# A perceiver layer on one core: the drain of the token loop without its 56 filler products

## The reference

```python
x = x + xattn(layernorm(x), ctx, ctx)   # 16 heads of 16, softmax(q k^T) v, output projection
x = x + attn(layernorm(x))              # rms norm, rotary q and k, sigmoid weights / their sum, v, projection
x = x + ffn(layernorm(x))               # one expert of 8 for each token, capacity 160 an expert, gelu, gate weight
```

## Time and profile before

| | us |
|---|---|
| median of 3 executions | 1117.71 |
| lowest, highest | 1116.65, 1118.75 |
| the profiled execution, its own time | 1113.46 |
| its span, first to last instruction | 1111.5 |
| its mean granted TensorE clock | 0.991 of full |
| PE, DVE, ACT, POOL busy in the span | 1073.4, 880.0, 798.7, 245.1 |
| the drain on PE, from the first hold to the first transposed row | 988.5 to 1020.3 |
| the experts, from there to the last product | 1020.3 to 1102.9 |

### The profile page before, as it was taken

The page is one execution under the profiler, slowest core; times in us unless marked ns, Lnnn a source line. Parts: engine busy times, 40 slices in busy tenths (PEclk is TensorE's granted clock), DMA queues, the critical chain, the costliest instruction groups (busy, mean ns, idle before and its releaser), DMA issues.

```text
span 1111.5 us, 40833 instructions
## 1 busy us (share of the span) xinstructions
PE 1073.4 (97%) x16195; PEld 875.3 (79%) x16195; DVE 880.0 (79%) x2650; ACT 798.7 (72%) x2319; POOL 245.1 (22%) x521
## 2 busy tenths in 40 slices
PE   6899999999999999999999999999999999988996
PEld 4678777878888888887887888888887788766996
DVE  6678888888888888888888888888888888774211
ACT  5677777887877877877888787787787787742221
POOL 1011122222222222222222222222222222221111
PEclk9899999999999999999999999999999999999998
DMA  4452522222212221122222211122112221001673
GB/s 137 115 149 55 200 67 69 69 65 62 62 46 58 59 63 54 45 59 60 62 61 60 61 58 43 55 59 57 44 52 58 58 60 36 17 12 44 211 244 109
DMA packets 71100, 82.04 MB, mean 74 GB/s; under 512 B 16427, under 2 KB 49916, under 8 KB 70912
## 3 DMA queue, kind: packets, MB, share of 16 engines
q1 hardware_dynamic: 64896, 75.06, 23.2%
q0 software_dynamic: 3360, 3.72, 1.0%
q10 hardware_dynamic: 2656, 0.66, 0.3%
HBM read 64.79 MB, written 16.56 MB: 73 GB/s over the span
## 4 chain that ended last, share of the span: by engine, by line
PE 85%; issue 4%; DVE 3%; DMA 3%; SPq 2%; ACT 1%; POOL 1%; POOLq 0%; DVEq 0%; ACTq 0%
PE vps L423 16%; PE kps L411 14%; PE score L457 9%; PE score L443 7%; PE gather L470 6%; PE shared L479 5%; PE shared L494 4%; PE shared L533 4%; PE score L766 3%; PE score L752 3%; PE shared L518 3%; PE shared L400 2%; PE score L485 2%; PE score L502 2%; SPq L266 1%
## 5 line engine op out<-in xcount | busy, mean ns | idle before, releaser
L818 ACT ACTIVATE prob<-score,nmx 128x257 f32<-128x257 f32 x512 | 236.2, 477 | 92.0 <-DVE nmx L1070 91.9
L411 PE MATMUL kps<-ctx_p,wk_p 128*128 128x512 f32 x768 | 217.3, 412 | 0.5 <-DVE wk_p L1056 0.4
L423 PE MATMUL vps<-wv_p,ctx_p 128*128 128x256 f32 x1536 | 215.7, 290 | 0.8 <-issue 0.8
L1070 DVE TENSOR_REDUCE nmx<-score 128x2 f32<-128x514 f32 x256 | 165.3, 688 | 54.6 <-PE score L443 54.6
L423 PEld LDWEIGHTS vps<-wv_p,ctx_p 128*128 128x128 f32 x1536 | 191.9, 190 | 15.2 <-issue 13.8
L411 PEld LDWEIGHTS kps<-ctx_p,wk_p 128*128 128x128 f32 x768 | 138.2, 190 | 38.7 <-issue 13.7
L1081 DVE TENSOR_SCALAR prob<-prob,rsum 128x256 f32<-128x256 f32 x512 | 159.4, 354 | 9.1
L1537 POOL TENSOR_TENSOR rstd<-ve,const 128x1 f32<-128x1 f32 x64 | 52.9, 826 | 464.4 <-DVE ve L1199 234.9
L457 PE MATMUL score<-const,prob 128*128 128x128 f32 x1024 | 147.1, 276 | 5.3 <-DVE prob L1081 5.0
L457 PEld LDWEIGHTS score<-const,prob 128*128 128x128 f32 x1024 | 115.6, 142 | 9.0 <-DVE prob L1081 7.6
L1062 DVE SCALAR_TENSOR_TENSOR ctx_p<-ctxT,nlast,ctx_p 128x256 fp32r<-128x256 f32 x256 | 111.8, 478 | 8.2 <-ACT ctx_p L835 8.2
(11 more groups left out here) (226 smaller groups left out, 1757.7 us busy)
## 6 DMA issues: line engine op xcount, KB each, us to landing
ctxT<-in_ctxT SPq DMA_DIRECT2D x128, 257.0 KB, 3.2
w<-in_w SPq DMA_DIRECT2D x16, 1024.0 KB, 8.8
xq<-in_x SPq DMA_DIRECT2D x32, 128.0 KB, 2.1
xr<-in_x SPq DMA_DIRECT2D x32, 128.0 KB
qbd<-qkT SPq DMA_DIRECT2D x248, 16.0 KB, 1.8
out<-row SPq DMA_DIRECT2D x31, 128.0 KB, 3.1
slots<-row SPq DMA_DIRECT2D x10, 257.0 KB, 5.7
x_a<-slots SPq DMA_DIRECT2D x8, 129.0 KB, 2.1
```

Of the source, the lines that this page charges most:

```text
L411: last = mm(kps[:, :], wk_p[:, x, n, c * P:(c + 1) * P], ctx_p[:, y, n, 2 * r:2 * r + 2, :].rearrange("p j s -> p (j s)"), start=(n, x) == ...
L423: last = mm(vps[:, c, :], ctx_p[:, x, n, j, c * P:(c + 1) * P], wv_p[:, y, n, :], start=(n, x) == (0, LO), stop=(n, y) == (C - 1, LO))
L818: last = af(prob[:, m, :], score[:, m, 0:S], ACT.Exp, bias=nmx[:, m:m + 1], scale=1.0, accum_out=esum[:, m:m + 1])
L1070: v.tensor_reduce(nmx[:, 2 * c:2 * c + 2], score[:, 2 * c:2 * c + 2, 0:S], AX.X, ALU.max, negate=True).then_inc(s["max_done"], 1)
```

## The change

The eight counts are set to zero, so that `hold` issues nothing. No wait, semaphore, buffer or other instruction changes.

```diff
-HOLDS = (12, 5, 2, 4, 5, 1, 3, 24)
+HOLDS = (0, 0, 0, 0, 0, 0, 0, 0)
```

## The result

| | before | after |
|---|---|---|
| median (lowest to highest), 6 executions each | 1117.08 (1113.02 to 1118.75) | 1125.97 (1123.54 to 1127.69) |
| ratio, 95% interval | | 1.0068 (1.0048 to 1.0087) |
| the profiled execution, its span | 1113.46, 1111.5 | 1127.69, 1125.6 |
| mean granted clock | 0.991 | 0.970 |

The kernel without the 56 products is slower, by 7.6 us by the ratio (5.4 to 9.7). The median lies 0.3 us above the top of the range that I gave (1125.7); the ratio, applied to the 1117.71 us that the range was built on, gives 1125.3, inside it. In the last series of experiments the changed kernel was timed again beside the other, six executions: 1.0060 (1.0038 to 1.0083), which is 6.7 us. Four executions in the experiments took 5% longer or more (1177.62, 1185.93, 1192.03 and 2948.37 us), and the ratios leave them out.

What follows compares the result with a forecast made beforehand. PE was taken to bound the token loop and, without cover, the experts; the drain alternates between engines. Terms -0.7 + 1.3 + 1.6 + 2.3 = +4.5 us, carried to the median, gave 1122.2 us; 8-in-10 range 1118.7 to 1125.7.

Steps and rivals of the forecast that it cites:

- Time given back by the holds: Drain and wait before the experts: removing the 56 unread products returns their time, -0.7 us (-0.2 small places, -0.5 last 24).
- 0.5 us comes back: Last 24 products, before expert 0's transposes: rows land by 1019.7, plus 0.1 us signal, so PE could start 0.5 us earlier.
- The projection at the lower level: Query and key projection behind y1 in the drain: clock falls to 1.2 GHz, 2.93 us instead of 1.64, +1.3 us.
- The rest of the drain: Values, self scores, outputs and gates behind the projection: +3.2 us if the clock stays low throughout, half taken, +1.6.
- low from y1 to the end: Rival: rest of drain too thin to lift the clock, which rises late in the experts too; +6.8 us, 1124.5 us, chance 0.14.
- The projection and the values are dense enough to lift it again: Step for the drain behind y1: clock returns there, then thin pieces lower it, so half of 3.2 us was taken.
- The first expert: Expert 0 begins at 1.2 GHz after over 6 us of idle PE: transposes +0.5, products +1.8 over 4 us, together +2.3.
- the main case: Clock low in a part of the drain and at expert 0's start: 1122.2 us, own range 1119.8 to 1124.3, chance 0.60.
- SP's load: Sign: the load of the 32 rows (line 348), before the experts, comes 2 to 4 us later.
- Only the last pause counts: Rival: clock stays up in the drain and falls only ahead of the experts; +1.6 us, 1119.3 us, chance 0.17.
- The holds don't keep the clock: Rival: clock behaves alike in either kernel, drain and experts only get time back; -0.7 us, 1117.0 us, chance 0.06.
- Faster: Rival: holds delay the chain before the experts; at most -8.3 us, 1109.4 us; chance 0.03 for over 0.2% faster.

## Why the prediction was right or wrong

**Direction and order of size: right.** Slower with a chance of 0.77, by clock and not by work; it forecast +4.5, the ratio says +7.6 (5.4 to 9.7), the second one +6.7. Three terms were wrong, all of them the same way, too low, so nothing cancelled. The range held because its upper end took in the price of the low clock throughout, though I had given that case 0.14. By terms, against the two traces of the changed kernel:

- *Time given back by the holds, -0.7.* Wrong, it is 0 where a run can tell. The step that failed is "0.5 us comes back" from the last 24. I took the DMA's 164 KB by 1019.7 for the landing, and 0.1 us for the signal, which no run shows. The signal comes later: with nothing in PE's way it is 1.97 us from the issue of the load to the first transpose, with the 24 in the way 2.02. The Trainium skill (DMA: Bandwidth & Descriptors, on the anatomy of one DMA) says of the other path of issue, GpSimd's, that most of a fixed 2.0 us is the confirmation behind the last byte; on SP's path the sum is like it here, 1.97 us, but less than half of it lies behind the traffic: 0.6 us from the 164 KB to the transpose in the kernel before, some 0.5 in the changed one. Of the three places flush with their successors the first gave nothing either: y1 is transposed 3.2 us after the positions in both. The other two can't be read, since the clock is low there.
- *The projection at the lower level, +1.3.* Right: 2.90 us against 1.64.
- *The rest of the drain, +1.6 as half of 3.2.* The price was near, the half was the error. The clock was low through all of it, as in the rival "low from y1 to the end", to which I gave 0.14. In the first trace the self scores start 2.05 us later than before, of which the projection is 1.3 and the rest 0.8, as worked out. The two together cost 0.9 more (I had 0.7), output A until the start of output Z 1.0 more, with DVE now waiting 0.77 us for PE (I had 0.5, with idle time behind it as cover), from there to gate Z 0.9, and 0.4 to the last positions. That is 3.9 for my 3.2. The sentence that failed is "The projection and the values are dense enough to lift it again". They didn't in either trace of the changed kernel, nor with only the last 24, where the clock came back 24.2 us into the drain and for 3.4 us only. With the five products of place 1 right behind the projection it came back 10.8 us into the drain (all but the first 12).
- *The first expert, +2.3.* Too small, it is +3.6 and +3.1. The transposes cost 0.45 as worked out, the products 2.6 instead of 1.8. The clock came back 5.4 us after their start, not 4; the sixteen products of line 752, most of them at the lower level, are 7.23 against 4.62. Of the first trace's 3.6, 0.5 is no clock at all but a late load near the end (0.61 us of idle time ahead of a transpose at 1101.0).

So the sum of the terms as measured is 0 + 1.3 + 3.9 + 3.1 to 3.6 = 8.3 to 8.8 us in the traces, and the rival's +6.8 was the better forecast. The own range of the main case, 1119.8 to 1124.3, isn't what the ends of its terms give (-0.7 + 1.3 + 0 + 1.2 to -0.7 + 1.3 + 3.2 + 3.5, 1119.5 to 1125.0).

Of the signs that I named, the projection (2.90) and the self scores (2.05 us late) came as written. SP's load came 5.2 us later into the drain and not 2 to 4, line 752 took 7.23 us and not 6.4, and the clock didn't fall a second time, since it had never come back.

**The other rivals.** *Only the last pause counts* falls by both traces of the changed kernel, low from y1 on, and the run with the first 12 alone shows that the pause at y1 isn't needed for a fall. The rule of the Trainium skill (TensorE: Matmul & The Clock Gate, on HAM oscillation), that pauses between bursts bring the clock down, is true of the gap ahead of y1 and, in the run without the last 24, of the one ahead of the experts, but in that with the first 12 alone the clock fell with no pause over 1.53 us; its half for throttled time lies a little above the projection (1 - 1.64/2.90 = 0.43). For line 752 it fits: of 7.23 us the last 1.87 ran at the upper level, so the first 5.36 did what takes 2.75, a loss of 0.49. My 0.44 was the wrong one of the two there. *The holds don't keep the clock* falls by the table: each row without the first 12, the last 24 or the middle has more time at 1.2 GHz, and a slower ratio, than the kernel before. *Faster* falls by the ratio, and by the 1.97 us above: the landing doesn't wait for the products.

What is not settled: how much of the ratio belongs to the middle 20 products (places 1 to 6). No run had them alone. Taking the first 12 away costs 2.0 us and the last 24 away 2.6, and all of them 7.6, so the middle and the joint effect have some 3 us between them. Two pairs of the table differ by the middle 20 alone: without the last 24 it is 1.0036 against 1.0023, without the first 12 it is 1.0040 against 1.0018. That is 1.5 and 2.5 us by the ratios, 1.1 and 1.8 by the traces, and neither is clear of the two intervals. Open too is why the clock came back within the drain in one of three traces without products there.

## What to carry to other kernels

In a stage where TensorE waits for others and works in short pieces, its clock is a resource like a buffer. Read the granted clock in windows before calling a product without a reader waste, and price what follows at both levels, as far as the next dense stretch. Such products are free only where they end before what they wait beside, and how long they take depends on the clock that they find (24 took 7.83 us and 6.82, five took 2.50 and 1.44): a count that is flush at the upper level stands in the way at the lower, and a count that is flush when the clock has fallen is too short when it hasn't.

## What the runs showed that I had not expected

- A thin stage of 30 us, with PE busy for 20.36 of 33.5 us, stayed at 1.2 GHz throughout in two traces of three; in the third (only the last 24) the clock came back for 3.4 us. PE looks busier there than it would at 2.4 GHz, since each piece is longer (the projection 2.90 us for 1.64).
- The bytes of a load are through well before its waiter goes on: in the kernel before about 160 KB had moved 1.4 us after the second load's issue, the transpose began at 2.0 us.
- Avoiding a low stretch late in the drain saved nothing, since only products that nobody reads and two small positions lay in it. Two falls of the same length, 3.4 us, cost 0.7 us of the drain where one came 18.4 us into it and nothing where it came at 23.9. So where a fall comes counts as well as how long it lasts.
